# Frequency-domain mixing on one core: the last group of four finished while the last column is mixed, and the merge of the edge columns moved to the end

## What is computed

```python
xf = jnp.fft.rfft2(x, axes=(1, 2), norm='ortho')        # 4 x 128 x 65 x 768, complex
xr, xi = real and imaginary part, as 8 blocks of 96 channels
o1r = relu(xr @ w1[0] - xi @ w1[1] + b1[0])
o1i = relu(xi @ w1[0] + xr @ w1[1] + b1[1])
o2r = softshrink(o1r @ w2[0] - o1i @ w2[1] + b2[0], 0.01)
o2i = softshrink(o1i @ w2[0] + o1r @ w2[1] + b2[1], 0.01)
out = jnp.fft.irfft2(o2r + 1j * o2i, s=(H, W), axes=(1, 2), norm='ortho') + x
```

## Time and profile before

| | |
|---|---|
| time, median of 3 runs | 5492.44 us (5489.49 to 5497.87) |
| the profiled execution | 5488.38 us, span 5486.1 us |
| PE busy | 5304.0 us, 97% of the span |
| DVE, ACT, POOL busy | 3679.3, 2225.7, 626.6 us |
| mean granted PE clock | 0.989 |
| DMA | 421.17 MB, mean 77 GB/s |

### The profile page before, as it was taken

The page is one execution under the profiler, slowest core; times in us unless marked ns, Lnnn a source line. Parts: engine busy times, 40 slices in busy tenths (PEclk is TensorE's granted clock), DMA queues, the critical chain, the costliest instruction groups (busy, mean ns, idle before and its releaser), DMA issues.

```text
span 5486.1 us, 112334 instructions
## 1 busy us (share of the span) xinstructions
PE 5304.0 (97%) x44352; PEld 4323.0 (79%) x44352; DVE 3679.3 (67%) x5859; ACT 2225.7 (41%) x3457; POOL 626.6 (11%) x420
## 2 busy tenths in 40 slices
PE   6999999999999999999999999999999999999998
PEld 5777887778777787777877778777778877787776
DVE  5676666676666766667667676676766766766665
ACT  3443434434344343444434444334434344343442
POOL 0110011110111101111011110111100111101111
PEclk9999999999999999999999999999999999999999
DMA  3331333312333123331133321333312333123311
GB/s 101 94 86 30 81 94 93 96 28 72 94 93 98 37 61 94 94 98 46 53 94 93 98 56 42 94 94 98 80 35 78 93 98 93 35 63 93 97 48 47
DMA packets 1065696, 421.17 MB, mean 77 GB/s; under 512 B 1062816, under 2 KB 1062944, under 8 KB 1065120
## 3 DMA queue, kind: packets, MB, share of 16 engines
q1 hardware_dynamic: 1060384, 411.62, 28.1%
q10 hardware_dynamic: 4736, 1.60, 0.1%
HBM read 210.26 MB, written 201.33 MB: 75 GB/s over the span
## 4 chain that ended last, share of the span: by engine, by line
issue 89%; POOL 11%; POOLq 0%; DVE 0%
POOL x L770 11%; POOLq L769 0%; POOLq L773 0%; DVE x L722 0%; POOLq L770 0%; POOLq L782 0%
## 5 line engine op out<-in xcount | busy, mean ns | idle before, releaser
L770 POOL TENSOR_TENSOR x<-shrink_or_v,x 128x480 f32<-128x480 f32 (+1 forms) x416 | 626.4, 1506 | 4850.5 <-DVE shrink_or_v L715 4809.5
L687 DVE TENSOR_TENSOR shrink_or_v<-ps,wts 128x768 f32<-128x768 f32 (+1 forms) x544 | 501.5, 922 | 991.0 <-PE ps L478 991.0
L397 PE MATMUL ps<-tab,ring_h 128*128 128x128 f32 x6144 | 741.1, 286 | 91.2 <-DVE ring_h L741 91.2
L478 PE MATMUL ps<-wts,hbig 128*128 128x192 f32 x4160 | 821.6, 340 | 0.0
L397 PEld LDWEIGHTS ps<-tab,ring_h 128*128 128x128 f32 x6144 | 735.0, 202 | 100.6 <-DVE ring_h L741 100.6
L478 PEld LDWEIGHTS ps<-wts,hbig 128*128 128x128 f32 x4160 | 661.0, 189 | 122.2 <-issue 122.2
L567 ACT COPY zbig<-ps 128x512 f32<-128x512 f32 (+1 forms) x544 | 308.8, 568 | 981.2 <-PE ps L413 981.2
L384 PE MATMUL ps<-tab,ring_a 128*64 128x128 f32 x6144 | 680.6, 273 | 3.7 <-ACT ring_a L536 3.6
L546 ACT COPY ydg<-ps 127x512 f32<-127x512 f32 (+5 forms) x896 | 502.4, 570 | 447.3 <-PE ps L397 278.4
L385 PE MATMUL ps<-tab,ring_a 128*63 128x128 f32 x6144 | 680.6, 273 | 0.0
L384 PEld LDWEIGHTS ps<-tab,ring_a 128*64 128x64 f32 x6144 | 671.4, 137 | 8.3 <-ACT ring_a L536 4.6
(11 more groups left out here) (52 smaller groups left out, 6594.8 us busy)
## 6 DMA issues: line engine op xcount, KB each, us to landing
x<-in_x SPq DMA_DIRECT2D x128, 1536.0 KB, 12.4
out<-x SPq DMA_DIRECT2D x352, 480.0 KB, 4.8
out<-x SPq DMA_DIRECT2D x32, 432.0 KB, 4.1
wts<-in_mix SPq DMA_DIRECT2D x16, 513.0 KB, 3.9
out<-x SPq DMA_DIRECT2D x32, 240.0 KB, 4.1
out<-x SPq DMA_DIRECT2D x32, 192.0 KB, 4.3
ydg<-row ACTq DMA_DIRECT2D x32, 48.0 KB
yedge<-row ACTq DMA_DIRECT2D x32, 0.8 KB
```

The costliest lines, as they stand in the source:

```text
L397: mm = pe.matmul(ps[:, line_bank(1, g), j * 128:(j + 1) * 128], ring_h[g % RING_H][:, j, :], mat("inv_h"), start=True, stop=True)
L478: mm = pe.matmul(o, hbig[u % 2][:, k * H:(k + 1) * H], mix_part("w2_big"), start=False, stop=True, skip_group_check=True)
L687: dve.tensor_tensor(parts(v), d, b2, ALU.add).then_inc(bias_done, 1)
L770: pool.tensor_tensor(xs[p][:, a:b, :], ucopy[g % 4][:, 0:b - a, :], mirror(xs[p], a, b), ALU.add).then_inc(plus_ready, 1)
```

## The change

Three things are changed. In `GROUP_PAIRS` the columns are dealt to the groups in another order: the last group of four now holds the columns 2 to 5 and the single one is column 1, so that the slots written late (2 to 11), together with the merged slots 0 and 1, are the first twelve of `ydg`; `LATE` is 12, ACT packs the slots 12 to 128, and DVE packs the slots 0 to 12. PE's pipelined loop now ends after turn 16, and the rest is written out by hand: second layer of group 15, first layer of group 16, merge, second layer of group 16. The merge leaves turn 5, writes to another bank (`E_BANK` is now the bank of the small transforms), and ACT's copy of it stands behind the last `relu` and ahead of the packs.

```diff
-GROUP_PAIRS = ([[(3, 4), (5, 6)], [(0, 64), (1, 2)]]
-               + [[(k, k + 1), (k + 2, k + 3)] for k in range(7, 63, 4)]
-               + [[(63, None)]])
+GROUP_PAIRS = ([[(6, 7), (8, 9)], [(0, 64), (62, 63)]]
+               + [[(k, k + 1), (k + 2, k + 3)] for k in range(10, 62, 4)]
+               + [[(2, 3), (4, 5)], [(1, None)]])
 NU = len(GROUP_PAIRS)
 EDGES = 1
-LATE = 2 * GROUP_PAIRS[NU - 2][0][0]
+
+LATE = 12
...
-        ZBIG_BANK, ZSMALL_BANK, BIG_BANK, SMALL_BANK, OUT_BANK, E_BANK = 0, 1, 2, 4, 5, 7
+        ZBIG_BANK, ZSMALL_BANK, BIG_BANK, SMALL_BANK, OUT_BANK, LAST_BANK = 0, 1, 2, 4, 5, 7
+        E_BANK = ZSMALL_BANK
...
-            return E_BANK if u == NU - 1 else OUT_BANK
+            return LAST_BANK if u == NU - 1 else OUT_BANK
...
                     pe.wait_ge(hid_ready, NU * q + u + 1)
-                    if u == NU - 1:
-                        pe.wait_ge(merged, q + 1)
-                    elif u:
+                    if 0 < u < NU - 1:
                         pe.wait_ge(bias_done, NU * q + u)
...
-                        for it in range(NU + 2):
-                            if it < NU:
-                                fwd_big(q, it)
+                        for it in range(NU):
+                            fwd_big(q, it)
                             if it == 1 and p == 0:
                                 pe.wait_ge(signs_set, t + 1)
-                            if 1 <= it < NU + 1:
+                            if it >= 1:
                                 mix1_whole(q, it - 1)
-                            if it < NU:
-                                fwd_small(q, it)
-                            if 1 <= it < NU + 1:
+                            fwd_small(q, it)
+                            if it >= 1:
                                 mix1_columns(q, it - 1)
                                 mix1_rows(q, it - 1)
                             if it >= 2:
                                 mix2_rows(q, it - 2)
                                 mix2_whole(q, it - 2)
-                            if it == EDGES + 4:
-                                merge(q)
+
+                        mix2_rows(q, NU - 2)
+                        mix2_whole(q, NU - 2)
+                        mix1_whole(q, NU - 1)
+                        mix1_columns(q, NU - 1)
+                        mix1_rows(q, NU - 1)
+                        merge(q)
+                        mix2_rows(q, NU - 1)
+                        mix2_whole(q, NU - 1)
                         inverse_lines(q)
...
                             if it >= 1:
                                 relu(q, it - 1)
-                            if it == EDGES + 5:
-                                act.wait_ge(merge_done, q + 1)
-                                act.copy(ydg[:, 0:2, :].rearrange("p k c -> p (k c)"),
-                                         ps[:, E_BANK, 0:2 * CB]).then_inc(merged, 1)
...
-                        act.wait_ge(merged, q + 1)
+                        act.wait_ge(merge_done, q + 1)
+                        act.copy(ydg[:, 0:2, :].rearrange("p k c -> p (k c)"),
+                                 ps[:, E_BANK, 0:2 * CB]).then_inc(merged, 1)
                         act.wait_ge(shrunk, NU * q + NU - 2)
                         for g in range(RING_H):
-                            act.copy(*pack_moves(g, 0, LATE)).then_inc(packed_act, 1)
+                            act.copy(*pack_moves(g, LATE, 128)).then_inc(packed_act, 1)
+                        act.wait_ge(merged, q + 1)
                         act.wait_ge(shrunk, NU * q + NU)
                         lines(q, p, 1)
...
                         for g in range(RING_H):
-                            dve.tensor_copy(*pack_moves(g, LATE, 128)).then_inc(tail_packed, 1)
+                            dve.tensor_copy(*pack_moves(g, 0, LATE)).then_inc(tail_packed, 1)
                         lines(q, p, 1)
```

## The result

The changed kernel takes 5477.66 us (median of 20 runs, 5473.94 to 5479.3); the kernel before takes 5492.91 us in the same comparison (20 runs, 5479.39 to 5503.16). The ratio is 0.9973, with a 95% interval of 0.9967 to 0.998: faster by 0.27%. Predicted were 5476 us. The spread says something too: 24 us before, 5 us after.

What follows compares the result with a forecast made beforehand. PE's work and waits bound the kernel, with DVE's pack delaying the inverse lines. 5488.4 + 1 (chain less merge) - 46.6 + 29.3 (low clock) = 5472.1, plus 4.06 to the median: 5476 us; forecast's own range 5463 to 5486, overall 5446 to 5494.

Steps and rivals of the forecast that it cites:

- The bound and the clock: Inverse lines: PE waits 2.85 us a pass for DVE's pack, and the lower clock costs 46.6 us of busy time.
- The merge leaves turn 5, -0.65 us: In turn 5 PE no longer does the merge, which saves 0.65 us a pass.
- The second layer of group 15, 0: At the mixing's end, moving it earlier gains 0: it still waits about 1.1 us for DVE's bias of group 14.
- The chain, +0.68 us a pass: Work behind group 15 delays DVE's start on group 16 by 0.68 us a pass, bounds +0.45 to +0.9 us.
- ACT hidden: At the mixing's end ACT's later packs cost 0, and the merge hides its relu of group 16 with 0.27 us to spare.
- The falls, 18 cheap ones and 29 us: Around the inverse lines 23 clock falls become 18, each costing 1.63 us, 29 us in all.
- the narrower spread (2.1 us of 2.75): Moments around PE's return when the clock can fall narrow from 2.75 to about 2.1 us; falls scale with it.
- the dear falls: Early clock falls that cost 2.6 us a pass in the inverse lines, in nine passes; they were to go.
- The sum, 5476 us: Whole kernel: 5472.1 us for a profiled execution, predicted as a median of 5476 us.
- The 4.06 us added to come to the median: Whole kernel: the median shown lies 4.06 us above the profiled execution, so this was added to 5472.1 us.
- Never falls any more: Rival: in the inverse lines the clock never falls, or in a handful of passes; 5447 us, chance 0.15.
- Slower, by a fall within the mixing: Rival: the clock falls within the mixing, +40 us on the forecast in ten passes, 5516 us; chance 0.12.

Runs made afterwards that it cites:

- e4: Kernel before plus nine useless matmuls a pass in PE's wait ahead of the inverse lines: 5443.9 us, ratio 0.9909.
- e3: Kernel before with the new dealing of columns and the merge moved to the end, PE's order otherwise old: 5444.7 us, ratio 0.9908.
- e7: Changed kernel with group 15's second layer written to banks 0 and 1 and the merge to bank 3: 5411.7 us, ratio 0.9854 to the kernel before.
- e2: Kernel before with only PE's order changed, group 15's second layer ahead of group 16's first, merge still in turn 5: 5500.1 us, ratio 1.0009.
- e12: Kernel before plus three useless matmuls a pass in PE's wait ahead of the inverse lines: 5466.8 us, ratio 0.9959.
- e8: e7 with the merge behind group 16's second layer and ACT's copy of it between its second and third packs: 5405.9 us, ratio 0.9846 to the kernel before.
- e10: e3 plus six useless matmuls a pass in PE's remaining wait: 5418.3 us, ratio 0.9865 to the kernel before.
- e1: Kernel before with only the new dealing of the columns, PE's order and merge unchanged: 5492.8 us, ratio 1.0.

## Why the prediction was right

**The bound and the clock.** Right. The forecast stood on the reading that the dear part of the wait was the lower clock after it (46.6 us), not the idle time. e4 shows it by itself. "Elsewhere PE is back to back" was put too strongly: two short waits, 17.8 and 14.9 us in 32 times each, stand in the list of before, but they are the same after the change.

**The merge leaves turn 5, -0.65 us.** Right; e3, where nothing else on PE moves, has it as a pure gain.

**The second layer of group 15, 0.** Right: PE waits 1.14 us for DVE's bias (I had 1.1), and group 15 is finished no earlier. e7 shows the cause, the shared banks.

**The chain, +0.68 us a pass.** The mechanism was right, the size somewhat low: 0.80 us, within the bounds given. The merge starts 3.70 us after group 15's second layer, as worked out, but the second layer of group 16 comes 0.85 us later instead of 0.75, since the merge's second matmul starts 0.43 us after the first (1013.30 - 1012.87) and not 0.32 as in e3. So the sum without the clock is +4.8 us, not +1.

**ACT hidden.** Right in the full change: its packs end 1014.04 + 5.47 = 1019.5, and PE waits for none. The relu of group 16 was hidden by the merge as said; e2, where the merge is not there, pays 0.46 us for it.

**The falls, 18 cheap ones and 29 us.** Twenty came, all cheap, 32.2 us. The estimate by the narrower spread (2.1 us of 2.75) was near for the wrong widths: falls came only between 0.5 us before the return and 1.0 after, 1.5 us apart, and yet in 20 of 32 passes. By the same scaling that width would give 12 or 13. The share of passes does not follow the width in proportion, then, and the number was lucky there. That the dear falls would go came true, but the reason given for it (PE is never idle for 1.5 us any more) is not borne out: e12, where PE still stands 2.19 us, has no dear fall, and e2, where it never stands longer than 1.44 us, has one.

**The sum, 5476 us.** Its closeness to 5477.66 us owes something to luck. The sum for a profiled execution, 5472.1 us, was 6.6 us too low (3.8 from the chain, 2.9 from the low clock). The 4.06 us added to come to the median belong to the kernel before, whose executions scatter; the changed kernel's median lies 1.0 us below its profiled execution (5478.67 us), so that term was 5.1 us too high, and the two errors nearly cancel.

**The rivals.** "Never falls any more" is out by the twelve and twenty passes. By the Trainium skill's page "TensorE: Matmul & The Clock Gate", section "HAM oscillation — how this bites in real kernels", long gaps between bursts should be what matters. These runs differ: with the same last wait of 1.44 us the clock fell in 20 passes (changed), in 25 (e2) and in 3 (e7), and with 0.79 us in 6 (e8). The changed kernel and e7 have the same matmuls ahead of that wait and differ in the other one, of 1.14 us, 5.7 us earlier; so the last wait alone does not decide it. That what lies ahead of it counts as well is the nearest reading and not shown by itself: the pass also became 1.2 us shorter in e7, and no run keeps its length and changes only what lies ahead. "Slower, by a fall within the mixing" did not occur: the mixing takes the same 103.33 us in every pass.

What the prediction did not ask is whether the parts pull the same way. They do not: the merge alone gives 48 us, and the order written out by hand takes 33 of them back; the profiled executions show 26 us of them as the 0.80 us a pass on the chain, and 3 as low clock.

## What to carry to other kernels

Where PE comes back from a regular short wait, look at the granted clock of the stage behind it: its price can be busy time that looks like work, and here it was half as large as the wait itself. Here, starting a group earlier brought nothing until what it writes to was free; look for the buffer or bank wait first, and move work into the wait that ends the stage rather than ahead of the work that its consumer needs. Take a change of several parts apart, even a successful one.

## What the runs showed of the hardware

- The clock fell to 1.2 GHz around waits of PE of 2.85, 2.2, 1.44 and even 0.79 us, and often not during the wait but up to 1.5 us after PE was back at work (in the kernel before, the inverse lines that began at 4582.17 have a clock of 0.83 from 4583 to 4584). What decides in which pass it falls is open.
- 2 us of useless matmuls a pass made the kernel 49 us faster; 0.7 us of them gave back about half of it.
- The kernels without a fall in their profile repeat within 0.6 to 1.8 us (e10 without the one execution named above); the kernel before, with 9 dear falls in its profile, spreads over 18 to 30 us in its four comparisons, and e1, with 12, over 21.
